# Two-layer transformer block: layer 0's query and key split by VectorE out of PSUM, and three changes in the order of work

## The reference, cut to what matters

```python
def _L0_attn_ref(x, w_qkv, w_out, b_out):
    qkv = (x @ w_qkv).reshape(B, T, 3, NUM_HEADS, HEAD_DIM)
    q, k, v = (qkv[:, :, 0], qkv[:, :, 1], qkv[:, :, 2])
    scores = jnp.einsum('bthd,bshd->bhts', q, k) / np.sqrt(HEAD_DIM).astype(np.float32)
    weights = jax.nn.softmax(scores, axis=-1)
    attn = jnp.einsum('bhts,bshd->bthd', weights, v).reshape(B, T, C)
    return attn @ w_out + b_out
...
x = L0_attn_x
xn = _layernorm(x, axis=-1)
x = x + _L0_attn_ref(xn, ...) + _L0_ffn_ref(xn, ...)
xn = _layernorm(x, axis=-1)
x = x + _L1_attn_ref(xn, ...) + _L1_ffn_ref(xn, ...)
```

## Time and profile before

| what | value |
|---|---|
| median of 3 runs | 1415.12 us (1406.73 to 1417.27) |
| the profiled execution, its own time | 1399.45 us |
| its span in the trace | 1397.7 us |
| mean granted clock of TensorE in it | 0.957 of full speed |
| turns 1 to 6, start to start | some 160 us each |

### The profile page before, as it was taken

One profiled execution on the slowest core, in us unless ns is written; L12 is line 12 of the kernel. 1 busy time (PEld: TensorE's weight loads), 2 busy tenths in 40 slices (PEclk: granted clock), 3 DMA queues, 4 the chain that ended last, 5 costly groups with the idle time before them and its releaser, 6 DMA issues.

```text
span 1397.7 us, 22040 instructions
## 1 busy us (share of the span) xinstructions
PE 1263.6 (90%) x7781; PEld 604.0 (43%) x7781; DVE 1040.5 (74%) x1922; ACT 805.4 (58%) x1314; POOL 406.6 (29%) x463
## 2 busy tenths in 40 slices
PE   2688699999999999999999999999999999999986
PEld 1213266334734256343643357243653347333641
DVE  7977888678886789768986788857886788724821
ACT  1155236864477735965478734876368734885455
POOL 3401332215231332315230342315222152205320
PEclk7669699999999999999999999999999999999988
DMA  4304383316714075224723167132733168105810
GB/s 120 111 2 123 111 241 107 102 50 210 221 37 127 30 257 168 92 67 153 233 79 110 39 221 207 58 109 89 251 116 100 48 211 219 31 1 162 247 50 8
DMA packets 120735, 171.77 MB, mean 123 GB/s; under 512 B 18153, under 2 KB 98354, under 8 KB 120626
## 3 DMA queue, kind: packets, MB, share of 16 engines
q0 software_dynamic: 27168, 90.44, 20.4%
q1 hardware_dynamic: 92514, 79.38, 19.6%
q10 hardware_dynamic: 944, 0.54, 0.1%
HBM read 116.88 MB, written 52.89 MB: 121 GB/s over the span
## 4 chain that ended last, share of the span: by engine, by line
PE 61%; DVE 22%; ACT 8%; DVEq 4%; issue 3%; DMA 2%; POOL 0%; ACTq 0%; POOLq 0%
DVE nm L978 12%; PE mx L1397 11%; PE sums L1389 11%; ACT ex L741 8%; PE ring L1270 8%; PE mx L1351 6%; PE sums L1486 6%; PE ring L1474 5%; PE ring L1265 3%; PE ring L1276 3%; DVE nm L982 2%; PE sums L1441 2%; PE ring L1329 2%; PE ring L1351 1%; PE ring L1463 1%
## 5 line engine op out<-in xcount | busy, mean ns | idle before, releaser
L741 ACT ACTIVATE ex<-mx 128x1024 f32<-128x1024 f32 x512 | 496.1, 1022 | 90.6 <-PE mx L1397 89.6
L978 DVE TENSOR_REDUCE nm<-mx 128x2 f32<-128x1024 f32 x422 | 493.9, 1217 | 66.6 <-PE mx L1351 66.6
L1397 PE MATMUL mx<-qs,ks 128*128 128x512 bf16 (+1 forms) x1024 | 281.9, 389 | 11.0 <-ACT ex L741 3.1
L762 ACT ACTIVATE ex<-ring,wx_sb 128x128 f32<-128x128 f32 x480 | 137.2, 368 | 174.9 <-PE ring L1474 169.8
L1351 PE MATMUL mx<-ks,qs 64*128 64x512 bf16 x844 | 158.8, 402 | 52.2 <-DVE nm L978 47.4
L1397 PEld LDWEIGHTS mx<-qs,ks 128*128 128x128 bf16 (+1 forms) x1024 | 78.3, 98 | 251.8 <-ACT ex L741 148.5
L579 POOL DMA_INDIRECT wx_sb<-wx,wx_row x120 | 114.7, 956 | 247.3 <-PE sums L1486 232.7
L982 DVE TENSOR_REDUCE nm<-ring 128x1 f32<-128x512 f32 x180 | 115.6, 683 | 30.5 <-PE ring L1351 29.6
L1389 PE MATMUL sums<-ex,vs 128*18 128x512 f32 x1024 | 137.4, 609 | 0.0
L1486 PE MATMUL sums<-wx_sb,ex 128*128 128x128 f32 x960 | 136.4, 285 | 0.0
L1474 PE MATMUL ring<-xsT,wx_sb 128*128 128x128 f32 x960 | 132.7, 282 | 4.0 <-issue 4.0
(11 more groups left out here) (191 smaller groups left out, 1396.4 us busy)
## 6 DMA issues: line engine op xcount, KB each, us to landing
scratch<-parts SPq DMA_DIRECT2D x64, 384.0 KB
ks<-scratch SPq DMA_DIRECT2D x256, 64.0 KB, 2.2
qs<-scratch SPq DMA_DIRECT2D x256, 64.0 KB, 2.2
scratch<-parts SPq DMA_DIRECT2D x32, 256.0 KB
xs<-x_sorted POOLq DMA_DIRECT2D x24, 256.0 KB, 7.2
o_sorted<-xs POOLq DMA_DIRECT2D x24, 256.0 KB, 4.2
rest<-parts SPq DMA_DIRECT2D x32, 128.0 KB
x_sb<-x SPq DMA_DIRECT2D x8, 256.0 KB, 4.0
```

What stands on the lines that cost most here:

```text
L741: act.activation(ex[:, ex_buffer(l, b, k), 2 * i:2 * i + 2, :], mx[bank][:, :, :], ACT.Exp, scale=SCALE).then_inc(mx_free[bank], 1)
L762: last = act.activation(ex[:, free_buffer(it, "tiles"), c, i % TG * P:i % TG * P + P], bank[:, c * P:(c + 1) * P], ACT.Silu, bias=wx_sb[n ...
L978: dve.tensor_reduce(nm[l][:, t, h:h + 2], mx[bank][:, :, :], AX.X, ALU.max, negate=True).then_inc(mx_free[bank], 1)
L1397: return pe.matmul(bank, ks[l][r, h, s * P:(s + 1) * P], qs[l][r, h, :], start=True, stop=True)
```

## The change

Layer 0's q0 and k0 are no longer copied by ACT. DVE casts them straight from the two banks of the ring, subtracts there, and frees the banks (`split_products`). The tiles' pairs of layer 1 are cut by rounding up, so that tiles 1 to 14 have 3,2,2,3,2,2,2,3,2,2,3,2,2,2. `place_maxima(2)` stands in front of `shared_hidden(part, it, 2)`. At the start, DVE's first piece of weights and the split wait for the first weight load alone, PE makes pairs 0 and 1 before the transposes of x, and slot 0 stands in front of the second half of the maxima's rows.

```diff
@@ maxima_of_tile
-    return [(1, pair) for pair in range(NPAIR * (i - steps) // (NTILE - steps), NPAIR * (i + 1 - steps) // (NTILE - steps))]
+    n = NTILE - steps
+    return [(1, pair) for pair in range((NPAIR * (i - steps) + n - 1) // n, (NPAIR * (i + 1 - steps) + n - 1) // n)]
@@ semaphores
-        weights_in, fp4_in = sem("weights_in"), sem("fp4_in")
+        weights_in, fp4_in = sem("weights_in"), [sem("fp4_first_in"), sem("fp4_rest_in")]
@@ ScalarE, turn
-                    if k == Q_SLOT and not last:
-                        qk_out(0, part, it, it + 1, 0)
-                    if k == K_SLOT and not last:
-                        qk_out(0, part, it, it + 1, 1)
@@ ScalarE, ahead
-                    act.dma_start(work[0:n, (a + c) * P:(a + c + 1) * P], w[f:f + n, :]).then_inc(fp4_in, 16)
-            act.dma_start(work[:, 6 * P:6 * P + F0], w_down).then_inc(fp4_in, 16)
+                    act.dma_start(work[0:n, (a + c) * P:(a + c + 1) * P], w[f:f + n, :]).then_inc(fp4_in[1 if a + c else 0], 16)
+            act.dma_start(work[:, 6 * P:6 * P + F0], w_down).then_inc(fp4_in[1], 16)
             copy_out("ahead", 0, "xT0", xnT[0][:, :])
-            qk_out(0, "ahead", 0, 0, 0)
-            qk_out(0, "ahead", 0, 0, 1)
...
             copy_out("ahead", 0, "m0_low", nm_hl[0:NH, :], rows=NH)
+            for k in range(LEAD):
+                exponentials(0, "ahead", 0, 0, k)
             act.wait_ge(low_rows_in, N_ROWS)
             copy_out("ahead", 0, "m0_high", nm_hl[0:NH, :], rows=NH)
-            for k in range(LEAD):
-                exponentials(0, "ahead", 0, 0, k)
@@ VectorE
+            def split_products(part, it, b):
+
+                wait(dve, scratch_out, (nth(0, b) - 1) * N_STORES)
+                wait(dve, p3_ready, nth(0, b) - 1)
+                banks = [from_ring(part, it, f"{'qk'[m]}0") for m in range(2)]
+                for m in range(2):
+                    dve.tensor_copy(parts[:, 0, m, :], banks[m][0][:, :])
+                dve.drain()
+                for m in range(2):
+                    dve.tensor_tensor(qk_f[:, m, :], banks[m][0][:, :], parts[:, 0, m, :], ALU.subtract).then_inc(banks[m][1], 1)
+                dve.drain()
+                dve.tensor_copy(parts[:, 1, :, :], qk_f[:, :, :]).then_inc(qk_split, 1)
@@ VectorE, turn
-                    for step in range(3):
-                        split_qk(0, part, it, it + 1, step)
+                    split_products(part, it, it + 1)
@@ VectorE, ahead
-            dve.wait_ge(fp4_in, 16 * N_FP4_DMAS)
+            dve.wait_ge(fp4_in[0], 16)
             dve.wait_ge(consts_set, 5)
             quantize_weights(0)
-            for step in range(3):
-                split_qk(0, "ahead", 0, 0, step)
+            split_products("ahead", 0, 0)
+            dve.wait_ge(fp4_in[1], 16 * (N_FP4_DMAS - 1))
@@ TensorE, turn
                 place_maxima(1)
+                place_maxima(2)
                 shared_hidden(part, it, 2)
-                place_maxima(2)
                 shared_hidden(part, it, 3)
@@ TensorE, ahead
-            quantized_x("ahead", 0, 0)
             for pair in range(2):
                 maxima(0, "ahead", 0, 0, pair)
+            quantized_x("ahead", 0, 0)
...
-            first_max_rows("m0_high", 2)
             pe.wait_ge(rest_in[0], 2 * N_STACK)
             pe.wait_ge(low_rows_in, N_ROWS)
             for k in range(LEAD):
                 slot_scores(0, "ahead", 0, k)
+            first_max_rows("m0_high", 2)
```

More of the change, by code:

```diff
@@ L708, in gates, with qk_out @@
                 act.activation(sg[:, t % 2, :], bank[:, 0:F0], ACT.Silu).then_inc(free, 1)
-            def qk_out(l, part, it, b, m):
+            def qk_out(part, it, b, m):
                 if m == 0:
-                    wait(act, p3_ready, nth(l, b) - 1)
-                if (l, m) == (0, 0) and part != "ahead":
-                    read_out(act, "turn", it - 1, ("up", NT - 1))
-                bank, free = from_ring(part, it, f"{'qk'[m]}{l}")
-                if l == 0:
-                    act.copy(qk_f[:, m, :], bank[:, :]).then_inc(free, 1)
-                else:
-                    act.activation(qk_f[:, m, :], bank[:, :], ACT.Identity, bias=bqk_sb[:, m:m + 1]).then_inc(free, 1)
+                    act.wait_ge(p3_ready, nth(1, b) - 1)
+                bank, free = from_ring(part, it, f"{'qk'[m]}1")
+                act.activation(qk_f[:, m, :], bank[:, :], ACT.Identity, bias=bqk_sb[:, m:m + 1]).then_inc(free, 1)
             def ffn_hidden(part, it, chunks):
@@ L809, in turn @@
                     if k == 8:
-                        qk_out(1, part, it, it, 0)
+                        qk_out(part, it, it, 0)
                     if k == 9:
-                        qk_out(1, part, it, it, 1)
+                        qk_out(part, it, it, 1)
                     if k == 10:
```

## The result

The changed kernel takes 1400.08 us (median of 11 runs, 1395.98 to 1409.83), the kernel before beside it 1410.42 us (11 runs, 1404.77 to 1417.27). The ratio is 0.9927, 95% interval 0.9907 to 0.9947: 10.3 us faster. The prediction was -1.7 us, 1413.4, with a range from 1403 to 1421. The time lies under that range; put on the median that the prediction started from, 1415.12, the ratio gives 1404.8, near its low end. The gain is under 1%, as the likeliest chance had it, and six times the sum.

What follows compares the result with a forecast made beforehand. No engine was taken as full, PE nearest at 90% busy and 61% of the chain that ended last. Terms 0 + 0.2 + 0 + 0 - 1.9 = -1.7 us took the median 1415.12 to 1413.4, range 1403 to 1421.

Steps and rivals of the forecast that it cites:

- ScalarE's relief: Two ACT copies of 0.59 us dropped per split: nothing won, as ACT then waits 0.59 longer for PE's scores.
- The pairs of the tiles: One pair moved from tile 14 to tile 1 in seven turns: +0.2 us in all, bounds -6.7 and +7.7.
- the waits in tile 1 and behind tile 14: Tile 1: third pair waits for DVE, tokens' transposes about 1 us later; tile 14: exponentials start right behind the table load.
- I take 0: q0/k0 split on VectorE: 0.84 us more DVE work each, hidden where DVE waits 8.58 for PE; bounds -8.3 and +5.9.
- -1.9: End of the start: slot 1's first exponential at 81.2 instead of 83.14 us; bounds -2.8 and -0.9.
- H2: Third shared product, behind the moved pair: 1.3 us late in turn 0, counted +0.9; three turns -0.3 each; sum 0.
- Rival 4: ACT's relief counts after all because slots run closer together: -10 us, 1405; chance 0.06.
- rival 1: Front of the tiles is free, idle DVE time taking up the lateness before tile 14: -8.2 us, 1407; chance 0.20.
- rival 2: Gain at the end, at tile 14, doesn't come and the kernel is slower: +6.7 us, 1422; chance 0.17.
- rival 5: At the start POOL's clearing doesn't hold DVE and the 2.51 us is won: -4.2 us, 1411; chance 0.07.
- the 2.51: DVE's wait in us for the last weight load at the start; most expected lost again under POOL's clearing, counted 0.
- rival 3: Banks come free too late and PE stands at hT0 until DVE's subtraction: +4.2 us, 1419; chance 0.10.

## Why the prediction was wrong

**Right: the mechanism of each step, in a turn without late ends.** ScalarE's relief is worth 0 (waits 0.70 to 1.19, the next exponentials at the same distance; and with the copies put back the time stayed). The split is 3.43 long and hT0 isn't held. The casts and subtractions out of PSUM took 0.68 and 0.69 each on VectorE, the copies 0.59 on ScalarE; so the rule of the Trainium skill that spoke against the edit (Advanced Engine Details and Errata, The Read-Write Bubble) agrees with the price, and the loss fell where VectorE waits. The pairs of the tiles (+0.15 a turn, 1.0001), `place_maxima(2)` (1.0012) and the waits in tile 1 and behind tile 14 are as worked out.

**Wrong: "I take 0" for the split.** Alone it gives 6.6 us by its ratio (2.1 to 11.2 by the interval, 4.4 by the medians). The step counted instructions by their durations and asked only which engine is late behind them. It did not ask what runs beside VectorE on GpSimd, and what a shift of a few tenths between the two would set off. 4.4 us of it are the late end in turn 1: that it goes with VectorE's list is shown by all these traces, that it goes by way of the held issue is argued from them, since no run changed that alone. The rest, some 2 us, is within the scatter of the late ends in the collecting: over turns 2 to 6 the profiles of the kernels with two transfers in flight both ways add up to 810.7 us (seven with the old split) and 807.3 (six others), too few and too scattered to settle it.

**Wrong: the size of the start.** "-1.9", with bounds -2.8 and -0.9. The order of events was right, the size was that of one exponential, and slot 1's came 1.2 earlier instead of 1.9. The clock's rise was in the bounds only as something that might fail to come; that it could come 9 us earlier and carry the whole stretch behind it was not. The rise alone is worth 4.2 us by the end of layer 0's attention in turn 0; start, rise and H2 together make 4.8 us up to turn 1 in the two profiles, the start 3.3 in runs and, with `place_maxima(2)`, 6.2.

**Wrong: the trace as a stand-in for the median.** "I work out a difference and put it on that median." The profiled execution lay 15.7 us under the median, and the text said that it couldn't tell why. It was the one of nine traces with the old split in which turn 1 had no late end, and no wait of it ended with "remote". A change that removes late ends can't be priced from an execution that has none. The median had its own error: of the 13.3 us between the forecast 1413.4 and the measured 1400.08, 4.7 are the kernel before itself, 1415.12 in three runs and 1410.42 in eleven.

**The rivals.** Rival 4 had the number (-10, 1405) and the wrong reason: ScalarE's relief, which two runs refute. Rivals 1, 2 and 5 fall with the pairs at 1.0001 and with VectorE's first steps still held by GpSimd's clearing (two of them 1.50 and 1.46 long, at 9.89 and 11.84; of the 2.51, 0.9 was won); rival 3 with hT0 unheld.

No version with the whole computation was clearly faster than the changed kernel: split and start without the rest are its equal, one transfer in flight is slower.

## What to carry to other kernels

If a profiled execution lies well under the median of the runs, first take a second profile of the same kernel and look for waits without a releaser; they show what the first one doesn't hold. Price an edit that adds or drops instructions also by what it shifts: find the neighbour engine's transfers that stand within half a microsecond of the engine that gets longer. Where indexed transfers overlap, treat TensorE's recorded ends beside them as estimates, and test the number in flight; and at a low clock, count what follows when an idle stretch of TensorE is closed, not only the stretch itself.

## What the runs showed of the hardware that was not expected

- TensorE's signals come up to some 6 us behind its recorded ends while GpSimd's indexed transfers overlap (with four in flight, scores that ended at 583.76 let ScalarE go on at 589.69): with one in flight never in the collecting, with two in some turns, with four in all. What holds them up is open. With all indexed transfers made plain, the kernel before is 25.5 us faster; some 2 us of that are the shorter sorting in the last turn (its first silu of the tiles stands 95.4 instead of 97.7 us into the turn, in the two traces of this kernel without a "remote" wait).
- An issue of an indexed transfer on GpSimd takes 0.96, and 1.83 when it starts 0.23 behind the start of VectorE's subtraction of 1.23 us with both inputs in SBUF. All 108 issues that began inside such a subtraction ended 0.83 or 0.84 behind its end, however late they began.
- VectorE pauses 0.2 us at one place of its instruction list, and this place moves with two instructions more a split. Where it stands ahead of the cast that starts the sorting, turn 1 is 4.4 us shorter (161.1 instead of 165.5).
- With 1.2 us of idle TensorE between 78 and 82 us closed, the rise from 1.2 to 2.4 GHz came at 84 to 89 us in eight profiles of nine; with that idle time it came at 93 to 97 in nine of eleven. An early rise alone was worth 4.2 us some 30 us later, and 1.2 us in the end, where the clock fell once more.
